# Attention column products in pieces of two inside quads 29 to 31 of the count loop, in place of whole blocks and unread products

## The reference, cut to what matters

```
h = x @ W + b
adj[row, col] = 1; adj[col, row] = 1; adj = adj + eye; adj = adj / row_sum
out = dw[0] * h; cur = h
for i in range(3): cur = adj @ cur; out = out + dw[i + 1] * cur
...
Wx = x @ Ws[h] + Wb[h]
s = Wx[v_tgt] @ a_w[h, :d] + Wx[v_src] @ a_w[h, d:] + a_b[h]
```

## Time and profile before

| | |
|---|---|
| median of 3 runs | 385.28 us (385.11 to 385.52) |
| the profiled execution's own time | 384.96 us |
| its span on the core | 383.1 us |
| PE busy | 368.6 us, 2740 matmuls |
| DVE busy | 277.6 us |
| ACT busy | 235.3 us |
| granted TensorE clock, mean | 0.991 of full speed |

### The profile page before, as it was taken

One profiled execution on the slowest core, in us unless ns is written; L12 is line 12 of the kernel. 1 busy time (PEld: TensorE's weight loads), 2 busy tenths in 40 slices (PEclk: granted clock), 3 DMA queues, 4 the chain that ended last, 5 costly groups with the idle time before them and its releaser, 6 DMA issues.

```text
span 383.1 us, 7752 instructions
## 1 busy us (share of the span) xinstructions
PE 368.6 (96%) x2740; PEld 217.2 (57%) x2740; DVE 277.6 (72%) x615; ACT 235.3 (61%) x402; POOL 100.5 (26%) x91
## 2 busy tenths in 40 slices
PE   8799999999999999999999999999999999999980
PEld 3355585444444444444444444444568889999980
DVE  7799988469976772226755445553995879999994
ACT  8999867678512444222651111478877999999235
POOL 3003000099700477001990000466300000121210
PEclk9999999999999999999999999999999999999996
DMA  5970050032000000000442000133203113110006
GB/s 167 385 234 0 3 204 18 2 124 95 2 0 0 1 2 3 0 2 1 88 91 41 0 0 2 28 79 75 41 0 115 56 55 113 56 57 3 2 3 222
DMA packets 27974, 22.70 MB, mean 59 GB/s; under 512 B 19552, under 2 KB 20768, under 8 KB 27936
## 3 DMA queue, kind: packets, MB, share of 16 engines
q1 hardware_dynamic: 27072, 19.06, 16.8%
q10 hardware_dynamic: 864, 3.15, 2.3%
HBM read 15.87 MB, written 2.13 MB: 47 GB/s over the span
## 4 chain that ended last, share of the span: by engine, by line
PE 88%; DVE 5%; ACT 4%; issue 2%; DVEq 0%; POOL 0%; POOLq 0%
PE ps L807 22%; PE ps L1212 10%; PE ps L1153 8%; PE ps L1054 7%; PE ps L1095 7%; PE ps L1017 7%; PE ps L1008 7%; PE ps L854 6%; PE ps L998 4%; PE ps L983 4%; PE ps L875 3%; ACT cts L518 2%; PE ps L930 1%; PE ps L895 1%; DVE early L1791 1%
## 5 line engine op out<-in xcount | busy, mean ns | idle before, releaser
L807 PE MATMUL ps<-big,xTs 128*128 128x512 f16 x384 | 84.3, 379 | 0.0
L807 PEld LDWEIGHTS ps<-big,xTs 128*128 128x128 f16 (+1 forms) x384 | 37.0, 98 | 43.4
L715 ACT ACTIVATE big<-big,uvt 128x1024 bf16<-128x1024 f32 x55 | 58.9, 1146 | 0.0
L616 ACT ACTIVATE big<-xcur,nmr,rstd (+1 forms) x24 | 19.5, 814 | 33.5 <-DVE nmr L1507 33.5
L447 POOL TENSOR_TENSOR big<-xcur,big x16 | 18.5, 1156 | 60.1 <-ACT xcur L617 59.2
L854 PE MATMUL ps<-big,xTs 128*128 128x512 f32 x64 | 32.6, 606 | 0.0
L464 POOL TENSOR_TENSOR xcur<-xcur,c 128x512 f32<-128x512 f32 (+2 forms) x8 | 8.9, 1107 | 88.1 <-DVE c L1710 83.4
L486 ACT ACTIVATE big<-ps 128x512 f16<-128x512 f32 (+1 forms) x16 | 9.4, 587 | 33.3 <-PE ps L807 30.9
L1153 PE MATMUL ps<-big,cst 128*128 128x260 f16 x256 | 29.8, 275 | 0.0
L1017 PE MATMUL ps<-big,adj 128*128 128x512 f16 x128 | 27.9, 379 | 0.0
L1054 PE MATMUL ps<-cst,big 128*128 128x512 f16 x128 | 27.8, 379 | 0.1
(11 more groups left out here) (233 smaller groups left out, 713.3 us busy)
## 6 DMA issues: line engine op xcount, KB each, us to landing
big<-u_rows ACTq DMA_DIRECT2D x6, 512.0 KB, 3.6
xcur<-in_x SPq DMA_DIRECT2D x1, 2048.0 KB, 16.9
out<-xcur SPq DMA_DIRECT2D x8, 256.0 KB, 2.3
big<-in_W SPq DMA_DIRECT2D x1, 1024.0 KB, 5.9
xTs<-in_xT SPq DMA_DIRECT2D x1, 1024.0 KB, 10.0
big<-in_W3T SPq DMA_DIRECT2D x1, 1024.0 KB, 12.6
xTs<-in_W1T SPq DMA_DIRECT2D x1, 1024.0 KB, 5.3
xTs<-in_wc SPq DMA_DIRECT2D x1, 1024.0 KB, 8.2
```

The costliest lines, as they stand in the source:

```text
L715: act.activation(above[:, a % AHEAD, :], uf[:, h % 2], ACT.Relu, scale=BIG, bias=vb[:, j, h:h + 1]).then_inc(S["above_in"], 1)
L807: return mm(bank, lhs(k)[a], rhs(k)[b], start=start and k == 0 and n == 0, stop=stop and k == KT - 1 and n == 2)
```

## The change

The blocks of attention columns become pieces: `attention_piece(k, j)` issues product `j` of block `k`. Behind each window of quads 29, 30 and 31 come two pieces, where one unread product was. That makes 12 products, blocks 0 to 2; block 3 keeps its place behind turned block 0. `COLUMNS_AT` is gone, and so nothing comes behind the parts of `h` in quad 28. The waits that each block had stand once, ahead of quad 29. The six unread products at the end stay.

```diff
-FILL_FROM, FILL = 29, (1, 6)
-COLUMNS_AT = {28: (0,), 29: (1,), 30: (2,)}
+COLUMNS_FROM, PIECES = 29, 2
+FILL = 6
...
                     ins.then_inc(S["win_done"], 1)
-                    if q >= FILL_FROM:
-                        fill(FILL[0])
+                    if q >= COLUMNS_FROM:
+                        p0 = (w - 2 * COLUMNS_FROM) * PIECES
+                        for i in range(p0, p0 + PIECES):
+                            attention_piece(i // KT, i % KT)
...
-            def attention_columns(k):
-
-                pe.wait_ge(S["w_in5"], 16)
-                pe.wait_ge(S["small_in"], SMALL)
-                pe.wait_ge(S["h_lo"], 5)
-                pe.wait_ge(S["acc0"], 5)
-                for j in range(KT):
-                    ins = mm(ps[:, 2, k * 64:k * 64 + VCOL + H], w3t[:, j, k * P:(k + 1) * P], abT[:, j, :],
-                             start=j == 0, stop=j == KT - 1)
-                if k == KT - 1:
+            def attention_piece(k, j):
+                ins = mm(ps[:, 2, k * 64:k * 64 + VCOL + H], w3t[:, j, k * P:(k + 1) * P], abT[:, j, :],
+                         start=j == 0, stop=j == KT - 1)
+                if k == KT - 1 and j == KT - 1:
                     ins.then_inc(S["wa_done"], 1)
...
             for q in range(NQ):
-                if q == FILL_FROM:
+                if q == COLUMNS_FROM:
+                    pe.wait_ge(S["w_in5"], 16)
+                    pe.wait_ge(S["small_in"], SMALL)
                     pe.wait_ge(S["acc0"], 5)
                     pe.wait_ge(S["h_lo"], 5)
                 quad(q)
...
-                for k in COLUMNS_AT.get(q, ()):
-                    attention_columns(k)
...
-            attention_columns(3)
+            for j in range(KT):
+                attention_piece(KT - 1, j)
             pe.wait_ge(S["win_free"], NG - 2)
             ct_block(2).then_inc(S["ct_done"], 1)
-            fill(FILL[1])
+            fill(FILL)
```

## The result

The changed kernel takes 388.39 us (386.31 to 388.67, 8 runs) against 385.29 us (385.11 to 385.54, 8 runs): ratio 1.0066, 95% interval 1.0047 to 1.0085, slower by 3.1 us. The forecast was 384.6 us and its range ended at 385.9. The profiled execution took 388.61 us, with a span of 386.8 us against 383.1.

The account below looks back on a forecast made before the run. The prediction took PE to bound the kernel. Removing six unread products gave −0.66 us, with the move to pieces and the entries taken as 0: 385.28 − 0.66 = 384.6 us, range 384.1 to 385.9.

Parts of the forecast that it names:

- What else is moved past: Between the change and the last products, no DMA or queue and nothing starting by the clock instead of PE: no cost.
- The unread products: Six unread products behind the windows of quads 29 to 31 removed, 0.11 us each on PE's chain: 0.66 us gained.
- The pieces: Attention products in quads 29 to 31: six pairs at 0.41 us equal three blocks, 2.46 us; worth nothing on PE.
- six entries: PE changing from f16 windows to f32 pieces six times: 0 to 0.30 us in all, taken as 0.
- DVE and ACT keep up: Around quads 29 to 31 and the turned blocks, both engines move earlier with PE, so PE waits for neither.
- Rival 1: Clock falls to 1.2 GHz at turned blocks and block 3, 54.2 to 57.1 us: 2.0 us lost, 386.6 us; chance 0.13.
- Rival 3: The 0.66 us are lost again at turned block 4 (ACT's eviction) or the end (DVE, ACT): 385.3 us; chance 0.05.
- The sum: Whole kernel: −0.66 us from the unread products, entries taken as 0, giving 384.6 us.

Follow-up runs that it names:

- b_m10: Kernel before the change, with ten products left out of the branch never taken: 388.43 us against 385.38, ratio 1.0069.
- a_p10: Changed kernel with ten products added to the branch never taken, against the kernel before: 384.62 us against 385.38, ratio 0.9983.
- p_only: Kernel before with the pieces, six unread products kept (two behind each quad), four products added to the never-taken branch: 385.02 us against 385.52, ratio 0.9994.
- a_nofill: Changed kernel without the six unread products at the end, 16 products added to the never-taken branch: 384.63 us against 385.52, ratio 0.9974.
- a_loop: Changed kernel with the sums of the never-taken branch written as loops: 384.02 us against the kernel before's 385.24, ratio 0.9968.
- b_loop: Kernel before with the sums of the never-taken branch written as loops: 384.73 us against 385.24, ratio 0.9985.
- a_m6: Changed kernel with six products left out of the never-taken branch, against the kernel before: 385.54 us against 385.52, ratio 1.0001.

## Why the prediction was wrong

- **The step that failed** is "What else is moved past. No DMA and no queue", with its sentence that nothing between there and the last products starts by the clock and not by PE. A removed instruction moves PE's whole stream behind it. The stream has its own fetches, and those after this taken branch start at the branch and take 6.9 to 7.2 us for two blocks whatever PE does in between. The runs b_m10 and a_p10 show this step alone: ten products that are never executed move the time from 385.4 to 388.4 and from 388.4 to 384.6 us. The profile had the hint, the 0.11 us of idle at 142.95 with no engine named, and I read it as nothing.
- **The unread products:** 0.66 us, right (a place-restored kernel gained it up to the turned blocks).
- **The pieces:** I priced a pair at 0.41 us and six entries at 0 to 0.30 us more. Measured 0.37 us, so they gain 0.2 us in all (p_only: 0.22), where I excluded more than 0.05. This term was mis-sized: I took half a block for a pair, and a pair between f16 windows costs less. Why it does, and whether the f32 loads set the pace as I wrote, no run shows.
- **DVE and ACT keep up:** right. PE waited for neither at the change, and ACT's two evictions of 60.01 us began at 59.14, sooner by the same 0.87 us as L980. DVE started quad 29's window at 50.74 (worked out: 50.8), L1420 at 55.13 (55.0), L1468 at 55.69 (55.5), and the first L980 came at 56.86 (57.07). That it is the pieces which free DVE, and the unread products are worth 0.28 us without them, I had not seen.
- **Rival 1**, the clock, came nearest with 386.6 us, though even its upper end, 388.1, lies below what was measured, and it had another place and mechanism. At its place the clock was 1.00, also without any unread product behind the loop (a_nofill). The rule of the Trainium skill that I weighed there ("TensorE: Matmul & The Clock Gate", Part 4, on transposes) cost nothing in this kernel. The clock fell at 145.6 us, as a consequence of PE's idle time, and made about 1.6 us of the loss.
- **Rival 3** had the shape, a gain present at 60 us and gone later, but I gave it 0.05 and only ends of zero gain; it named ACT and the end, not a branch.
- **The sum**, −0.66 us, is near what the change is worth without the fetch: 0.71 us in the runs and 0.70 in the profiles (a_loop against b_loop). That is partly luck, since it left out the 0.2 us of the pieces. That a_p10's 384.62 us agrees with the forecast 384.6 is luck too: its profile keeps only 0.40 us, since it still idles 0.56 us at the branch. None of this makes the forecast of this kernel right.

## What to carry to other kernels

Where a change alters the number of instructions on an engine, look at every taken branch behind it and at any idle time there whose reason is "issue". Compare two kernels only with the place of the branch's target held, by code that is never executed; else a change worth −0.7 us is judged by +3. Even then the gap ahead of the first product can differ: a_p10 lost half of its gain there in its profile, and only the pair without the gap (a_loop, b_loop) showed the change whole. Keep what a branch jumps over short, for instance by writing the rare path as loops: here that was worth 0.5 us to the old kernel and 4.4 us to the new one.

## What the runs showed of the hardware

- After PE's taken branch over some 540 instructions, its first block was usable 3.6 us (kernel before) to 4.1 us after the flag read. The packet of the next block came 3.1 to 4.2 us behind the first one's, and that block was usable after 6.9 to 7.2 us. With some 150 instructions jumped over, none of it showed; lengths between were not run. The Trainium skill ("Runtime: NRT & Kernel Launch", Instruction fetch mechanics) calls the cost of a boundary "mostly hidden". Here it was hidden with 36 products between target and boundary, partly with 10, and not with 4: 2.06 us.
- The granted clock fell to 1.2 GHz at 145.6 us, after PE had been idle for 0.65 us, had worked for 1.02 us and had been idle again for 1.8 us, and it stayed there for 3.4 us. Idle times of 0.36 and 0.74 us with 2.32 us of work between them (a_m6) left the clock at 1.00.
- A pair of f32 pieces of 40 columns between f16 windows costs 0.37 us, half a block of eight matmuls 0.41 us.
